# Four layers with low-rank parts on one core: VectorE's splits of S2 and S4 move around the gating, the turning and h2's sum move on TensorE, two x splits move among W3's tiles

## The reference, cut to what matters

```python
x = x + L0(x)   # x @ w_eff.T: 8-level quantised weight, scales per 128 inputs, rank-64 update
x = x + L1(x)   # x @ W1.T + 2 * sum over 8 experts of gate_e * (x @ A_e.T) @ B_e.T; two gates not zero
x = x + L2(x)   # x @ W2.T + b + 2 * (x @ As[id2]) @ Bs[id2]: one rank-16 adapter per sequence
x = x + L3(x)   # x @ W3[id3].T: one of 16 full 1024 x 1024 weights per sequence
```

## Time and profile before

| what | value |
| --- | --- |
| median of 3 runs (lowest, highest) | 660.65 us (659.86, 660.75) |
| the profiled execution's own time | 662.03 us |
| its span in the profile | 660.2 us |
| TensorE busy | 647.4 us, 98% |
| VectorE busy | 498.5 us, 76% |
| ScalarE busy | 365.1 us, 55% |
| GpSimd busy | 85.9 us, 13% |
| chain that ended last | TensorE 93%, VectorE 4%, ScalarE 1%, DMA 1% |

### The profile page before, as it was taken

How to read it: one execution, slowest core, us unless ns; L and a number is a source line. 1 busy time by engine, 2 the same in 40 slices (tenths; PEclk the granted TensorE clock), 3 DMA queues, 4 the chain that set the end, 5 groups by cost and what they waited for, 6 DMA issues and landing times.

```text
span 660.2 us, 10322 instructions
## 1 busy us (share of the span) xinstructions
PE 647.4 (98%) x3992; PEld 594.3 (90%) x3992; DVE 498.5 (76%) x645; ACT 365.1 (55%) x549; POOL 85.9 (13%) x120
## 2 busy tenths in 40 slices
PE   8999999999999998899999999999999999999997
PEld 8989989999999998899879999879999888999886
DVE  5799899879970549867878966878975978974753
ACT  6664573971911443645665754665664766563553
POOL 2320225004010010001210001221001112000010
PEclk9999999999999999899999999999999999999999
DMA  9762112111012002022664212566213486002372
GB/s 278 199 199 76 53 32 65 33 41 50 8 54 74 1 1 87 1 91 64 198 224 152 65 38 92 187 228 184 65 34 96 134 263 200 2 1 65 119 232 95
DMA packets 46020, 67.32 MB, mean 102 GB/s; under 512 B 3604, under 2 KB 32020, under 8 KB 45972
## 3 DMA queue, kind: packets, MB, share of 16 engines
q1 hardware_dynamic: 40900, 58.28, 28.2%
q10 hardware_dynamic: 5072, 8.39, 3.8%
HBM read 58.27 MB, written 8.39 MB: 101 GB/s over the span
## 4 chain that ended last, share of the span: by engine, by line
PE 93%; DVE 4%; issue 1%; ACT 1%; DMA 1%; DVEq 0%; ACTq 0%
PE ps L1258 29%; PE ps L1260 29%; PE ps L1259 29%; PE ps L1401 3%; PE ps L1269 1%; PE ps L1430 1%; DVE e_both L897 1%; PE ps L1403 1%; DMA xraw<-lora_a 1%; DVE x_both L897 0%; ACT ring_hi L670 0%; DVE e_mid_w L1178 0%; DVE e_both_w L1176 0%; DVE e_mid_w L1181 0%; ACT e_both L771 0%
## 5 line engine op out<-in xcount | busy, mean ns | idle before, releaser
L1258 PE MATMUL ps<-e_both,ring_hi 128*128 128x384 f32 (+3 forms) x384 | 133.5, 348 | 0.0
L1260 PE MATMUL ps<-e_both,ring_lo 128*128 128x384 f32 (+3 forms) x384 | 133.4, 347 | 0.0
L1259 PE MATMUL ps<-x_both,e_both 128*128 128x256 f32 x448 | 126.3, 282 | 0.0
L771 ACT ACTIVATE e_both<-raw 128x512 fp32r<-128x512 f32 x128 | 79.0, 629 | 72.7 <-PE ps L1260 72.3
L897 DVE TENSOR_TENSOR e_both<-raw,e_both 128x512 fp32r<-128x512 f32 x128 | 88.8, 721 | 39.2 <-ACT e_both L771 38.7
L1258 PE MATMUL ps<-e_both,e_mid 128*128 128x512 f32 (+2 forms) x288 | 110.9, 385 | 2.4 <-DVE e_both L897 2.4
L1260 PE MATMUL ps<-e_both,e_mid 128*128 128x512 f32 (+2 forms) x288 | 110.7, 384 | 0.0
L1259 PE MATMUL ps<-e_both,e_mid 128*128 128x512 f32 (+2 forms) x288 | 110.5, 384 | 0.0
L587 POOL TENSOR_TENSOR raw<-raw,ident 128x128 f32<-128x128 f32 x64 | 38.0, 595 | 366.2 <-DMA raw<-w_t 366.2
L1259 PEld LDWEIGHTS ps<-x_both,e_both 128*128 128x128 f32 x448 | 85.4, 191 | 0.0
L1260 PEld LDWEIGHTS ps<-e_both,ring_lo 128*128 128x128 f32 x384 | 72.2, 188 | 5.7
(11 more groups left out here) (175 smaller groups left out, 1279.9 us busy)
## 6 DMA issues: line engine op xcount, KB each, us to landing
raw<-w_t SPq DMA_DIRECT2D x64, 512.0 KB, 4.3
w_w<-x_t SPq DMA_DIRECT2D x16, 512.0 KB, 3.7
w_w<-w SPq DMA_DIRECT2D x15, 512.0 KB, 4.2
y<-tmp ACTq DMA_DIRECT2D x30, 256.0 KB, 4.0
e_both_w<-w_t SPq DMA_DIRECT2D x5, 512.0 KB, 8.1
e_both_w<-w_t SPq DMA_DIRECT2D x4, 384.0 KB, 6.4
e_mid_w<-bs SPq DMA_DIRECT2D x24, 64.0 KB, 3.7
e_mid_w<-b_cat SPq DMA_DIRECT2D x4, 128.0 KB, 6.3
```

Of the source, the lines that this page charges most:

```text
L771: act.activation(w3_ring_hi[(2 * k + h) % 4], raw[:, k % RAW, h * 512:(h + 1) * 512], ACT.Copy).then_inc(w3_hi, 1)
L1258: pe.matmul(out, a[0], b_[0], start=start, stop=False, **kw)
L1259: pe.matmul(out, a[0], b_[1], start=False, stop=False, **kw)
L1260: return pe.matmul(out, a[1], b_[0], start=False, stop=stop, **kw)
```

## The change

VectorE's halves of S2 now stand in front of the gating, its halves of S4 between the gating's first and second part. ScalarE's copy of h2's columns moves behind its bias copies, and its Exp behind its halves of S4. On TensorE the two turnings come after product 3 (before: after product 2), and h2_add after product 4 (before: after product 3); h2_add writes PSUM bank 6 in place of 5 and so waits for ScalarE to have copied the turned h2 out of that bank; product 5 no longer waits for h2's sum. Among the W3 tiles of the second sequence VectorE's low halves of T1 and T2 come after tiles 5 and 6, where ScalarE already had its copies.

```diff
@@ ScalarE, group @@
                 split_x(g, "T3")
-                act.wait_ge(tok_done, g + 1)
-                act.wait_ge(h2_clear, 1)
-                for j in range(2):
-                    act.activation(h2_tok[:, 2 * j:2 * j + 2, R2 * j:R2 * (j + 1)],
-                                   tok[:, 2 * j:2 * j + 2, NOW_AT[j]:NOW_AT[j] + R2], ACT.Copy).then_inc(h2_tok_done, 1)
-                act.wait_ge(gate, GATE_STEPS * g + GATE_DV)
-                act.activation(gw[:, 1, :], gw[:, 0, :], ACT.Exp).then_inc(e_exp, 1)
                 split_weight(g, "S2")
...
                     act.activation(bs_half[h], bs_raw[:, h * 512:(h + 1) * 512], ACT.Copy).then_inc(bs_hi1, 1)
+                act.wait_ge(tok_done, g + 1)
+                act.wait_ge(h2_clear, 1)
+                for j in range(2):
+                    act.activation(h2_tok[:, 2 * j:2 * j + 2, R2 * j:R2 * (j + 1)],
+                                   tok[:, 2 * j:2 * j + 2, NOW_AT[j]:NOW_AT[j] + R2], ACT.Copy).then_inc(h2_tok_done, 1)
                 split_weight(g, "S4")
+                act.wait_ge(gate, GATE_STEPS * g + GATE_DV)
+                act.activation(gw[:, 1, :], gw[:, 0, :], ACT.Exp).then_inc(e_exp, 1)
@@ VectorE, gating @@
                 assert n[0] == GATE_DV
 
+                split_weight(g, "S4")
                 dve.wait_ge(e_exp, g + 1)
@@ VectorE, group @@
                 dve.tensor_tensor(s4_whole, weight[0][1], s2_whole, ALU.subtract).then_inc(e_add, 1)
+                split_weight(g, "S2")
                 gating(g)
                 split_x(g, "T3")
-                split_weight(g, "S2")
...
                 dve.tensor_tensor(s3_whole, weight[0][0], weight[1][0], ALU.subtract).then_inc(e_add, 1)
-                split_weight(g, "S4")
...
                 for k in range(KT):
                     split_w3(g, 1, k)
-                    if k < 6 and not last:
+                    if k < 4 and not last:
                         split_x(g + 1, X_OPS[k])
+                    elif 5 <= k < 7 and not last:
+                        split_x(g + 1, X_OPS[k - 1])
@@ TensorE, h2_add and group @@
                 pe.wait_ge(gt_done, g + 1)
+                pe.wait_ge(h2_turned, 4 * (g + 1))
...
-                    pe.matmul(ps[0:64, 5, cols], br_now[:, j, :], gt_hi[:, cols], start=j == 0, stop=False,
+                    pe.matmul(ps[0:64, 6, cols], br_now[:, j, :], gt_hi[:, cols], start=j == 0, stop=False,
...
                 block_product(g, 2, False)
+                pe.wait_ge(c_copy, 4 * g + 2)
+                block_product(g, 3, False)
                 turn_h2(g)
                 turn_g(g)
-                pe.wait_ge(c_copy, 4 * g + 2)
-                block_product(g, 3, False)
-                h2_add(g)
                 pe.wait_ge(c_copy, 4 * g + 3)
                 block_product(g, 4, False)
-                pe.wait_ge(h2_summed, 2 * (g + 1))
+                h2_add(g)
                 block_product(g, 5, True)
```

More of the change, by code:

```diff
@@ L1200, in group @@
                 for i in range(2):
-                    dve.scalar_tensor_tensor(out=h2_sum, in0=ps[32 * i:32 * (i + 1), 5, :], scalar=2.0, in1=h2_sum,
+                    dve.scalar_tensor_tensor(out=h2_sum, in0=ps[32 * i:32 * (i + 1), 6, :], scalar=2.0, in1=h2_sum,
                                              op0=ALU.mult, op1=ALU.add).then_inc(h2_summed, 1)
@@ L1451, in h2_add @@
                 pe.wait_ge(gt_done, g + 1)
+                pe.wait_ge(h2_turned, 4 * (g + 1))
                 for j in range(2):
                     cols = slice(2 * j * P, 2 * (j + 1) * P)
-                    pe.matmul(ps[0:64, 5, cols], br_now[:, j, :], gt_hi[:, cols], start=j == 0, stop=False,
+                    pe.matmul(ps[0:64, 6, cols], br_now[:, j, :], gt_hi[:, cols], start=j == 0, stop=False,
                               skip_group_check=True)
-                    ins = pe.matmul(ps[0:32, 5, cols], br_now[:, j, 0:2 * R2], gt_lo[:, cols], start=False, stop=True,
+                    ins = pe.matmul(ps[0:32, 6, cols], br_now[:, j, 0:2 * R2], gt_lo[:, cols], start=False, stop=True,
                                     skip_group_check=True)
```

## The result

The changed kernel takes 673.78 us (median of 4 runs, 671.88 to 676.14); the kernel before, run beside it, 660.40 (659.86 to 660.75). The ratio is 1.0206, with a 95% interval of 1.0179 to 1.0232: slower, and 3.2 us less so than the forecast of 677.0. The profiled launch took 674.16 us (span 672.4).

A forecast was written before the change was run, and what follows sets the result against it. TensorE, busy 98% of the span, was taken to bound the kernel. Waits of 7.4 + 12.0 less gains of 6.8 and 2.9 give +9.7, clock falls 6.6: 660.65 + 16.3 = 677.0 us, range 668 to 686.

The forecast's parts named there:

- S2 ahead of the gating: Group 0, ahead of product 2: the 5.12 us wait and the half clock (1.66) go, gain 6.8 us.
- T1 and T2: W3 product of the second sequence, groups 0 to 2: three short TensorE waits go, gain 2.9 us.
- S3: Ahead of product 4: S3's low halves late, waits of 2.18 us in group 0, 1.74 in three others; loss 7.4.
- A12: Ahead of product 5: A12's halves stand behind h2's sum, which waits for h2_add; 3.0 us in four groups, 12.0 us.
- The halves of A22: With the W3 tiles, they follow product ends and move with them; no loss was counted.
- The clock: TensorE's clock falls to half in four new waits, at 1.66 us a fall; loss 6.6 us.
- a fall in each 3.0 us wait: Ahead of product 5: the clock falls in each of the four A12 waits, four falls, 6.6 us.
- no fall came at the waits of 1.7 to 2.1 us: Ahead of product 4: no clock fall in S3's waits of 1.7 to 2.2 us, which lie at the 2.09 us bound.
- Without falls: Rival: both new waits come but the clock stays full, 670.4 us; chance 0.2.
- Eight falls: Rival: the clock falls in S3's waits ahead of product 4 as well, 683.7 us; chance 0.2.
- S3 on time: Rival: S3 is not late for product 4, VectorE's list being 2 us shorter; 669.6 us with four falls; chance 0.1.
- A12 never started ahead of h2_add: Sign of the faster rival: A12's halves start before h2_add's end, only gains are left, 651.0 us; chance 0.04.

The follow-up runs named there:

- all_ahead: both_ahead plus ScalarE's `keep` ahead of S3's halves, VectorE's S3 difference ahead of T3's low part, A22 ahead of h2's last copy and low part: 649.87 us.
- a12_ahead: The changed kernel with one edit: VectorE splits A12 ahead of h2's sum, not behind it; 660.78 us, ratio 1.001.
- s3_ahead: The changed kernel with one edit: VectorE splits S3 ahead of the two small low parts and T4; 673.49 us, ratio 1.0208.
- both_ahead: The changed kernel with A12 split ahead of h2's sum and S3 ahead of the small low parts and T4; 659.46 us, ratio 0.9995.

## Why the prediction was right

*S2 ahead of the gating, gain 6.8 us.* Right: no wait ahead of product 2, and the half clock behind it gone. all_ahead, which has this gain and that of T1 and T2 and no wait, stands 10.1 us below before, against 6.8 + 2.9 = 9.7. S2's part was not run alone; its size is read from the traces.

*T1 and T2, gain 2.9 us.* Right: 2.6 us measured alone.

*S3, loss 7.4 us.* Right in place, and 0.7 low in size: 8.1. VectorE's list took 16.67 us where the sum of pieces said 16.51. What the prediction did not see is the second bound. Of ScalarE's list it weighed only the two parts that moved; `keep` was 0.31 us behind S3, so that putting right S3 alone gained only that. For the forecast this did no harm, since the later bound sets the wait.

*A12, loss 12.0 us.* Right in place and size: 2.99 and 3.00 us a group, and a12_ahead gave the 12 us and their falls back. The halves of A22 were said to follow product ends; that held in the changed kernel, where product 5 starts late, and failed when A12's wait was taken away.

*The clock, loss 6.6 us.* This is the mis-sized term. Three falls in the profiled launch, not four, at 1.5 us and not 1.66. The number changes from launch to launch: the four runs have mean clocks of 0.997, 0.994, 0.992 and 0.989 at 671.88, 673.40, 674.16 and 676.14 us. The profile with 0.992 has three falls, and one fall of 3.41 us takes 0.0025 off the mean, so these are one, two, three and four. The prediction took the time that TensorE had stood, 2.09 us in the earlier trace rows, for what decides; equal waits with and without a fall, and the fall 1.45 us into product 5, speak against that. That no fall came at the waits of 1.7 to 2.1 us was right for this profile, but by luck: a12_ahead has one at such a wait in group 0, the clock falling 1.36 us after product 4 had begun:

```profile
275.09:278.50 3.41, 3.41 (x18) 3.41 (x17) 2.59 (x3) 1.66 (x2) 0.00 (x0) 0.50 0.02 5
```

So "a fall in each 3.0 us wait" was the upper end of what happened, and the median lies 3.2 us below 677.0.

*The rivals.* Without falls it was to be 670.4 us; the quickest run was 671.88, with one fall. With 1.5 us for each of one to four falls the sum of the waits gives 671.9, 673.4, 674.9 and 676.4 us, within 0.8 us of the four runs: as a sum the waits were right, and what was off was the count of falls and their price. Eight falls and S3 on time did not happen, and A12 never started ahead of h2_add.

## What to carry to other kernels

When an instruction is moved up in an in-order list, write down what is now behind its wait, on that engine and on the next one; here a 5 us wait for S2 pushed 16.5 us of work down to S3's place. When a producer (h2_add) is moved down to just before a consumer, everything in the second engine's list between the two becomes exposed; moving the consumer's own preparation (A12) ahead of it costs one line. And a wait in the profile names only its latest cause: s3_ahead took 0.31 us off a wait of 1.9, as the next bound stood right behind, so look for the second bound before expecting a wait's whole length back.

## What the runs showed of the hardware

The same wait of 2.84 us of idle TensorE lowers the clock in some places of one launch and not in others, and the number of falls differs between launches of one program; why it falls here and not there is open. The price of one fall can be read from run times alone: in both_ahead the runs at a mean clock of 1.000 took 659.05 to 659.46 us and those at 0.997 took 660.59 to 661.06, 1.6 us apart on average, and in a12_ahead the same two kinds lie 1.3 us apart. all_ahead, with no wait left, stayed at 1.000 in all five runs, within 0.7 us of each other.
